# Low-rank weight products and the first rotations change engines in the opening stretch of a decoder kernel

## The reference, cut to what matters

```python
k = (c_kv @ Wk_up)...                      # and q = x @ Wq
q_rope, k_rope = _apply_rope(q_rope, ...), _apply_rope(k_rope, ...)
...
gate = einsum('btd,edf->ebtf', x, Wg)
gate = gate.at[:NL].add(einsum('btd,edr,erf->ebtf', x, Ga, Gb))   # up and out likewise, NL = 2, r = 64
```

## Time and profile before

| | before |
|---|---|
| median of 3 runs | 1698.6 us (1692.5 to 1699.74) |
| the profiled execution's own time | 1692.4 us |
| its span | 1690.6 us |
| PE busy | 1443.2 us, 85% |
| DVE busy | 1273.0 us, 75% |
| ACT busy | 903.6 us, 53% |
| POOL busy | 846.8 us, 50% |

### The profile page before, as it was taken

One profiled execution on the slowest core, in us unless ns is written; L12 is line 12 of the kernel. 1 busy time (PEld: TensorE's weight loads), 2 busy tenths in 40 slices (PEclk: granted clock), 3 DMA queues, 4 the chain that ended last, 5 costly groups with the idle time before them and its releaser, 6 DMA issues.

```text
span 1690.6 us, 26867 instructions
## 1 busy us (share of the span) xinstructions
PE 1443.2 (85%) x9924; PEld 869.5 (51%) x9924; DVE 1273.0 (75%) x2115; ACT 903.6 (53%) x1431; POOL 846.8 (50%) x724
## 2 busy tenths in 40 slices
...
GB/s 282 26 200 2 28 51 2 28 26 27 100 51 50 26 70 32 51 63 13 25 26 38 26 26 29 35 26 26 37 26 31 33 26 26 38 26 26 13 1 100
DMA packets 63105, 74.62 MB, mean 44 GB/s; under 512 B 6912, under 2 KB 40320, under 8 KB 61952
## 3 DMA queue, kind: packets, MB, share of 16 engines
...
## 4 chain that ended last, share of the span: by engine, by line
PE 60%; DVE 24%; issue 11%; ACT 3%; POOL 2%; DMA 1%; SPq 0%; DVEq 0%; POOLq 0%; ACTq 0%
PE banks L1103 48%; PE banks L870 6%; DVE nmf L1473 5%; DVE plo L1487 2%; PE banks L935 1%; DVE cat L1456 1%; PE banks L923 1%; DVE top L1599 1%; DVE wk L1595 1%; DVE att L1497 1%; DVE kcT L1463 1%; DMA w_fold<-w_top 1%; DVE attf L1606 1%; PE banks L1058 1%; DVE qcT L1483 1%
## 5 line engine op out<-in xcount | busy, mean ns | idle before, releaser
L1103 PE MATMUL banks<-xc,w 128*128 128x512 f16 x2688 | 591.2, 382 | 17.7 <-ACT banks L1144 15.0
L1103 PEld LDWEIGHTS banks<-xc,w 128*128 128x128 f16 x2688 | 264.2, 99 | 339.2 <-ACT banks L1144 20.2
L1103 PE MATMUL banks<-wd,mid 128*128 128x256 f16 x2688 | 298.1, 273 | 5.4 <-ACT banks L1144 3.1
L1103 PEld LDWEIGHTS banks<-wd,mid 128*128 128x128 f16 x2688 | 263.6, 98 | 40.9 <-ACT banks L1144 3.4
L847 POOL TENSOR_TENSOR mid<-m,mid 128x512 f16<-128x512 f32 x64 | 75.1, 1174 | 318.2 <-ACT mid L1144 318.2
L753 POOL TENSOR_TENSOR plo<-pf,phi 128x896 f16<-128x896 f32 x64 | 133.5, 2088 | 175.3 <-ACT phi L1144 175.2
L1144 ACT ACTIVATE banks<-banks 128x512 f32<-128x512 f32 x192 | 108.7, 579 | 193.0 <-PE banks L1103 193.0
L847 POOL TENSOR_TENSOR mid<-msum,mid 128x512 f16<-128x512 f32 x128 | 186.4, 1475 | 2.6 <-ACT mid L1144 2.6
L1421 DVE SCALAR_TENSOR_TENSOR w<-stage,w 128x512 f16<-128x512 f32 (+1 forms) x56 | 61.5, 1138 | 106.0 <-ACT w L1144 106.0
L1144 ACT ACTIVATE mid<-msum 128x512 f16<-128x512 f32 x128 | 81.2, 635 | 84.1 <-DVE msum L1780 28.1
L1473 DVE TENSOR_REDUCE nmf<-banks 128x1 f32<-128x512 f32 (+3 forms) x256 | 107.3, 480 | 14.9 <-PE banks L937 14.4
...
## 6 DMA issues: line engine op xcount, KB each, us to landing
...
```

The costliest lines, as they stand in the source:

```text
L1103: mm = nc.tensor.matmul(out, l(x, i), r(y, i), start=start and i == 0 and j == 0, stop=stop and i == k - 1 and j == 2, skip_group_check=True)
```

## The change

Six things change, all in the opening stretch.

1. The table in `kcT` is made in a small tile `own_small` of 4x16 and then spread to 4x8192 by one POOL copy.
2. A product leaves PSUM by ACT: `move_product` copies the four banks, scaled, into `product[n % 2]`, which lies in `pf` or in the new tile `low_high` (the old `phi` and `plo` in one). PE's next product waits for these copies (`lora_out`).
3. POOL adds a product to its weight with one instruction of 128x2048 (`lora_added` now counts 6, not 24). ACT's `move_product(n)` waits for the add of product n-2, and ACT's first batch waits for all six.
4. The eight rotations of the first batch are DVE's: `turn_row` has POOL's four instructions. Later batches keep POOL's.
5. The three tables of the opening stretch are written in another order.
6. The five later stores go in order 1 to 5, and each pair of factors shares a semaphore.

```diff
 A_START_PE = steps("""
-    xT.0 xT.1 xT.2 xT.3 turn.0 turn.1 row.0 c.0 row.1 fold.0 row.2 v.0 row.3 turn.2 fold.1 row.4 v.1 turn.3 fold.2 v.2
-    row.5 turn.4 fold.3 row.6 turn.5 fold.4 row.7 fold.5
+    xT.0 xT.1 xT.2 xT.3 turn.0 turn.1 row.0 c.0 fold.0 row.1 row.2 turn.2 v.0 row.3 fold.1 turn.3 row.4 v.1 fold.2 turn.4 row.5
+    v.2 row.6 fold.3 turn.5 row.7 fold.4 fold.5
 """)
 A_START_ACT = steps("""
-    fold.0 fold.1 row.0 c.0 row.1 rhi.0 row.2 rhi.1 row.3 v.0 fold.2 rhi.2 row.4 rhi.3 v.1 fold.3 v.2 row.5 rhi.4 fold.4
-    row.6 rhi.5 fold.5 row.7 rhi.6 rhi.7 v.3
+    half.0 half.1 row.0 c.0 row.1 rhi.0 fold.0 row.2 rhi.1 half.2 row.3 v.0 fold.1 rhi.2 row.4 half.3 rhi.3 v.1 fold.2 row.5 v.2
+    half.4 rhi.4 fold.3 row.6 half.5 rhi.5 row.7 rhi.6 fold.4 rhi.7 fold.5 v.3
 """)
 A_START_DVE = steps("""
-    half.0 half.1 c.0 rlo.0 rlo.1 fold.0 v.0 rlo.2 half.2 fold.1 v.1 rlo.3 half.3 fold.2 v.2 rlo.4 half.4 fold.3 rlo.5
-    half.5 fold.4 fold.5 cat0.0 cat0.1 cat0.2 cat0.3 cat0.4 rlo.6 cat0.5 rlo.7 cat0.6 cat0.7 maxn.0 maxn.1 maxn.2
-    maxn.3 v.3 mTn.0 maxn.4
+    half.0 half.1 rope.0 c.0 rope.1 rlo.0 half.2 v.0 rope.2 rlo.1 rope.3 rlo.2 half.3 v.1 rope.4 rlo.3 half.4
+    v.2 rope.5 rlo.4 rope.6 rlo.5 half.5 rope.7 cat0.0 rlo.6 cat0.1 cat0.2 cat0.3 rlo.7 cat0.4 cat0.5 cat0.6 cat0.7 maxn.0 maxn.1 maxn.2 maxn.3 v.3 mTn.0 maxn.4
 """)
...
         nm16 = sb(sa, "nm16", [P, TT, P], F16)
+        own_small = sb(sa, "own_small", [P, H], F16)
         qcT = sb(sa, "qcT", [P, H, S], F16)
...
         pf = sb(sa, "pf", [P, 2, TRI])
-        phi = sb(sa, "phi", [P, 2, TRI], F16)
-        plo = sb(sa, "plo", [P, 2, TRI], F16)
+        low_high = sb(sa, "low_high", [P, 4, TRI], F16)
+        phi, plo = low_high[:, 0:2], low_high[:, 2:4]
         osb = sb(sa, "osb", [P, 2, G, TT, 65])
...
         w_cat = vcat[:, :, :, :].rearrange("p h t n -> p (h t n)").bitcast(F32)[:, 0:2048].rearrange("p (t n) -> p t n", t=4)
+        product = [raw.rearrange("p a n -> p (a n)")[:, 0:2048].rearrange("p (t n) -> p t n", t=4) for raw in (pf[:, :, :], low_high[:, :, :].bitcast(F32))]
         w_raw = [w_cat, w_top[:, 0], w_top[:, 1], w_top[:, 2], x_res[:, :, :], att[:, :, :]]
...
         x2_kept = sem("x2_kept")
-        la_loaded = [sem(f"la{n}_loaded") for n in range(6)]
-        lb_loaded = [sem(f"lb{n}_loaded") for n in range(6)]
+        factors_loaded = [sem(f"factors{n}_loaded") for n in range(6)]
         wf_loaded = [sem(f"wf{n}_loaded") for n in range(6)]
...
         lora_mm = sem("lora_mm")
+        lora_out = sem("lora_out")
         lora_added = sem("lora_added")
...
             move_values(0, 1)
-            for n in (5, 4, 1, 2, 3):
+            for n in range(1, 6):
                 store_fold(n)
...
 
-            own_row = kcT[K3:K3 + G, :, :].rearrange("p (g j) n -> p g j n", j=G)
+            own_row = own_small[K3:K3 + G, :].rearrange("p (g j) -> p g j", j=G)
             pool.wait_ge(consts, 14)
-            pool.memset(kcT[K3:K3 + G, :, :], 0.0).then_inc(own_rows, 1)
+            pool.memset(own_small[K3:K3 + G, :], 0.0).then_inc(own_rows, 1)
             pool.wait_ge(own_rows, 1)
             pool.affine_select(out=own_row, in_=own_row, compare_op=ALU.not_equal, fill=SNM, base=0,
-                               pattern=[[0, H // G], [-1, G], [0, S]], channel_multiplier=1).then_inc(own_rows, 1)
-
+                               pattern=[[0, H // G], [-1, G]], channel_multiplier=1).then_inc(own_rows, 1)
             pool.wait_ge(own_rows, 2)
+            nc.gpsimd.tensor_copy(kcT[K3:K3 + G, :, :], own_small[K3:K3 + G, :].unsqueeze(2).to_broadcast([G, H, S])).then_inc(own_rows, 1)
+            pool.wait_ge(own_rows, 3)
+            for n in range(6):
+                pool.wait_ge(wf_loaded[n], 16)
+                pool.wait_ge(lora_out, 4 * (n + 1))
+                nc.gpsimd.tensor_tensor(w_raw[n], w_raw[n], product[n % 2], ALU.add).then_inc(lora_added, 1)
             pool.wait_ge(cossin_loaded, 16)
...
 
-            heads(next_part(A_POOL, A_NEXT), None, 0)
             with pool.Fori(0, B - 1) as b:
...
             def turn_factor(n):
-                pe.wait_ge(la_loaded[n], 16)
+                pe.wait_ge(factors_loaded[n], 32)
                 if n >= 2:
...
                     if n:
-                        pe.wait_ge(lora_added, 4 * (n - 1) + t + 1)
+                        pe.wait_ge(lora_out, 4 * (n - 1) + t + 1)
                     three(banks[:, t, :], lambda x, i: laT[:, n % 2, x, ts], lambda y, i: lb16[:, n % 2, y, :], 1, lora_mm)
...
             at = next_part(A_PE, A_NEXT).index(("cat0", 0))
-            pe.wait_ge(lora_added, 24)
+            pe.wait_ge(lora_out, 24)
             heads(next_part(A_PE, A_NEXT), None, 0, [], at)
...
             def factor_halves(n):
-                act.wait_ge(lb_loaded[n], 16)
+                act.wait_ge(factors_loaded[n], 32)
                 if n >= 2:
...
 
+            def move_product(n):
+                if n == 0:
+                    act.wait_ge(w_lo, 4)
+                elif n >= 2:
+                    act.wait_ge(lora_added, n - 1)
+                for t in range(4):
+                    act.wait_ge(lora_mm, 4 * n + t + 1)
+                    scaled(product[n % 2][:, t], banks[:, t, :], 1.0 / (SW * SW)).then_inc(lora_out, 1)
+
             for u in A_START_ACT:
                 if u[0] == "fold":
-                    if u[1] == 2:
-                        act.wait_ge(w_lo, 4)
+                    move_product(u[1])
+                elif u[0] == "half":
                     factor_halves(u[1])
...
                     heads([u], None, 0)
+            act.wait_ge(lora_added, 6)
             heads(own_part(A_ACT, ("res", "ln")), 0, 1)
...
 
-            def add_product(n):
-                dve.wait_ge(wf_loaded[n], 16)
-                for t in range(4):
-                    dve.wait_ge(lora_mm, 4 * n + t + 1)
-                    stt(out=w_raw[n][:, t], in0=banks[:, t, :], scalar=1.0 / (SW * SW), in1=w_raw[n][:, t],
-                        op0=ALU.mult, op1=ALU.add).then_inc(lora_added, 1)
+            def turn_row(i):
+
+                t = i // 2
+                if i == 0:
+                    dve.wait_ge(cossin_loaded, 16)
+                dve.wait_ge(a_drained["row"], a_upto(0, ("row", i)))
+                dve.wait_ge(roped, i * 4 + FREE)
+                pair = rows[:, i % 4, :, NOPE:HD].rearrange("p h (i two) -> p h i two", two=2)
+                for j, dst in ((0, turn_a), (1, turn_b)):
+                    cs = cossin[:, j, t].unsqueeze(1).to_broadcast([P, H, ROPE // 2, 2])
+                    tt_(dst[:, :, :, :], pair, cs, ALU.mult).then_inc(roped, 1)
+                dve.wait_ge(roped, i * 4 + (2 + FREE))
+                half = NOPE + ROPE // 2
+                tt_(rows[:, i % 4, :, NOPE:half], turn_a[:, :, :, 0], turn_a[:, :, :, 1], ALU.subtract).then_inc(roped, 1)
+                tt_(rows[:, i % 4, :, half:HD], turn_b[:, :, :, 1], turn_b[:, :, :, 0], ALU.add).then_inc(roped, 1)
 
             for u in A_START_DVE:
-                if u[0] == "half":
+                if u[0] == "rope":
+                    turn_row(u[1])
+                elif u[0] == "half":
                     factor_lows(u[1])
-                elif u[0] == "fold":
-                    add_product(u[1])
                 else:
```

More of the change, by code:

```diff
@@ L592, in _ @@
                 la, lb = (a[name][n // 3] for name in LORA[n % 3])
-                sp.dma_start(la_raw[:, n], la.rearrange("(t p) r -> p t r", p=P)).then_inc(la_loaded[n], 16)
-                sp.dma_start(lb_raw[:, n], lb).then_inc(lb_loaded[n], 16)
+                sp.dma_start(la_raw[:, n], la.rearrange("(t p) r -> p t r", p=P)).then_inc(factors_loaded[n], 16)
+                sp.dma_start(lb_raw[:, n], lb).then_inc(factors_loaded[n], 16)
                 if n % 2:
@@ L612, in store_fold @@
             def store_fold(n):
-                sp.wait_ge(lora_added, 4 * (n + 1))
+                sp.wait_ge(lora_added, n + 1)
                 sp.dma_start(w_fold[n // 3, n % 3].rearrange("(t p) n -> p t n", p=P), w_raw[n])\
@@ L948, in heads @@
                         if i == 0:
-                            pe.wait_ge(own_rows, 2)
+                            pe.wait_ge(own_rows, 3)
                         if i % G == 0:
```

## The result

| | before | changed |
|---|---|---|
| median, same session | 1699.17 us (4 runs, 1692.5 to 1702.38) | 1715.76 us (4 runs, 1709.07 to 1720.67) |
| ratio of the two, 95% interval | | 1.0102 [1.0066, 1.0138] |
| the profiled execution | 1692.4 us, span 1690.6 | 1709.07 us, span 1707.3 |
| `v.3` drained | 90.75 | 111.60 |

The change makes the kernel slower by 1.0%, 16.6 us between the medians. The forecast was 12.4 us and 1708.2; 1715.76 is near the upper end of its range, 1697 to 1717. A second session gave the same kernel a median of 1717.46, just over that end, and 1.0117 [1.0092, 1.0143] of its own before.

A forecast was written before the change was run, and what follows sets the result against it. The prediction took the end of `v.3`, with five stores behind it in SyncE's queue, as the bound. Its terms, -5.6 -1.3 +14.7 +3.6 +1.0, gave +12.4 us on 1695.8: 1708.2 us, range 1697 to 1717.

The forecast's parts named there:

- term 1: Opening table: POOL's copy ends before DVE's `wq` starts, so `wq` ends at 18.5 instead of 24.15: -5.6 us.
- term 2: DVE's own work in the opening: 24 adds go (14.73 us), eight rotations come (13.4 us): -1.3 us.
- term 3: SBUF path shared by POOL and DVE: POOL's additions stop DVE's two-input operations, 18.0 us for 3.3 before: +14.7 us.
- term 4: DVE's idle time from `wq` to the last `cat0` copy: 17.1 us for 13.5 before: +3.6 us.
- term 5: TensorE's clock in the heads' maxima, a ring of PE and DVE: two early rounds also at 1.2 GHz: +1.0 us.
- What bounds it: Opening stretch: five stores stand behind `v.3` in SyncE's queue, so the time moves by as much as `v.3`'s end.
- slow copy: Rival on the opening table: POOL's copy takes 16.4 us, `wq` ends at 26.8, time 1716.5 us; chance 0.06.
- The base: Time the forecast change was added to: 1695.8 us, the mean of two pairs of executions of the kernel before.
- the stalls fall off the path in part: Rival: stalls at `half.2` and `rope.2` (6.2 us) are absorbed; sum +6.2, 1702 us, no telling change; chance 0.22.
- hold nothing: Rival: POOL's additions hold nothing that DVE needs, so no stalls; 1692 us, no change; chance 0.05.
- Faster: Rival: DVE's waits swallow all its stalls in the opening; -10.2 us, 1685.6 us; chance 0.07.
- The clock, inside the forecast: Rival: PE's clock falls in its 5.9 us gap before `row.6`, costing 1.3 to 2.5 us more; no chance given.

The follow-up runs named there:

- e9: The changed kernel with its five later stores issued ahead of SyncE's wait for `v.3`: 1699.33 us, 1.0005 of the kernel before.
- e2: The kernel before with its five later stores issued ahead of SyncE's wait for `v.3`: 1686.76 us, 0.9924 of the kernel before.
- e1: The kernel before with only the table's change (small tile, one spreading POOL copy): 1692.02 us, 0.9957 of the kernel before.
- e4: The changed kernel with each POOL addition split into four pieces of 128x512: 1711.82 us, 1.0079 of the kernel before.
- e6: The kernel before with the table's change and the first batch's rotations on DVE, additions still on DVE: 1704.22 us, 1.0037 of the kernel before.
- e7: The changed kernel with the rotations back on POOL, between its additions: 1712.94 us, 1.0103 of the kernel before.
- e3: The changed kernel with POOL's six additions replaced by memsets about as long, which only write SBUF: 1695.38 us, 0.9991 of the kernel before.
- e10: The changed kernel with 56 extra matmuls in three of PE's gaps, none ahead of `cat0.3`: 1700.99 us, 1.0029 of the kernel before.
- e5: The changed kernel with 74 extra matmuls in four of PE's gaps, results thrown away: 1708.08 us, 1.0051 of the kernel before.
- e11: The kernel before with the table's change, stores ahead of `v.3` and 36 extra matmuls in PE's gaps: 1668.47 us, 0.9834 of the kernel before.

## Why the prediction was right, and where it was off

| from | forecast | measured, profiled execution |
|---|---|---|
| term 1, table | -5.6 | -5.7 |
| term 2, DVE's own work | -1.3 | -1.9 |
| term 3, stalls | +14.7 | +10.5 |
| term 4, DVE's idle time | +3.6 | +16.5 |
| term 5, clock in the ring | +1.0 | +1.4 |
| end of `v.3` | +12.4 | +20.8 |

- **What bounds it** held for the change, though not only through the queue. `v.3` came 20.85 us later and DVE went on 20.83 later. The stores behind `v.3` are worth some 14 us of DVE's wait in either kernel (18.5 for 4.3 behind `v.3`, e9), but with them out of the way a later `v.3` still cost its time (e9 over e2: 12.6 us for 14.6), since the lists of DVE and PE have it ahead of the first batch. "The time moves by as much as `v.3`" holds within the scatter behind it for the changed kernel, 16.6 and 20.2 us in two sessions for 20.85 and 21.2, and for e1, e4, e6 and e7. It does not for e3 (-3.4 for +3.2), e10 (+3.8 for +16.7) and e5 (+9.3 for +20.8), and why is open.
- **Term 1** held in the changed kernel and alone (e1). The slow copy, 16.4 us, is out with 7.01.
- **Term 2**, here what is left of DVE's busy time when term 3 is taken off: a rotation is 0.55, 0.55, 0.36 and 0.35, overlapping, close to the estimate.
- **Term 3** was right in its mechanism (e3) and too high for this execution. In the groups of the stretch the eight `turn_a` have a mean of 1498 ns for 550, `cat` 1026 for 690, `kcT` 1252 for 673: 7.6, 2.7 and 3.5, together 13.8 against 18.0, less the 3.3 of before. The missing stall is that of `rlo.3`. It ran from 50.95 to 51.63, and addition 2, forecast at 51.0, came at 53.81, since `fold.2` was slow. In its place the first operation of `half.4` lost 0.9, and `rlo.6` lost 2.7 for 3.9. With the clock held, addition 2 comes at 51.14 and the stall is there. The additions took 4.50 to 4.59 where I had taken 4.4; the row of another shape with 9% for fp32 was a little low. The Trainium skill's 4497 ns for 2048 fp32 columns (GPSIMD Engine Reference, "Elementwise — side-by-side cycle accounting") was the closer figure, and the trace agrees with it; by it the sum of the prediction, by its own estimate, would have been 0.5 us more.
- **Term 4 is the step that failed.** "17.1" was 29.9. The forecast's wait for `half.2` (2.6) was met at 2.60; not forecast was the 5.62 ahead of `half.4`, the wait for `rope.6` was 7.15 for 4.5, and those in the `cat0` steps 9.1 for 4.7. In each of the three PE is at a product of 5.30 us. The prediction had named the gap and the price, "may cost 1.3 to 2.5 more", for one gap, and left it outside the sum. There were four gaps of 3.4 to 4.8 us, three of them right behind a stall, and three products of 2.76 took 2.54 more each, with shorter groups beside them. e5 and e10 show that this is the cause up to `cat0.0`: with the clock held it comes at 76.97, for 82.93 without, and `rlo.6` within 0.8 us of its place in the forecast. e10's DVE had 20.9 us of idle time, 3.8 over the forecast, 2.9 of it in the copies behind `cat0.0`, at the low clock. In the end of `v.3` e10 won back 4.2 of the 8.4 us that the forecast missed; most of the other half lies behind `cat0.0`, where no run held the clock.
- **Term 5** had the right rows and was 0.4 low: all three rounds between the four maxima took 3.45, the first maximum came 2.60 behind the last `cat0` copy's start for 1.88, and the 0.4 taken off for overlap wasn't there.
- **The base**: the mean of the four executions, 1695.8, was 3.4 under the median that the session gave, 1699.17. Both errors have one sign; together they are the 7.6 us between 1708.2 and 1715.76. That this lies inside the range is in part luck: `v.3` was 8.4 us past its forecast, and the first session gave 4.2 of them back in the scatter behind it. The second session's 1717.46 is half a microsecond outside.
- **The rivals**: that the stalls fall off the path in part, or hold nothing, is refuted by e3, which takes out only the reading and gets 17.6 us back. (Its "3.7 before today's `v.3`" can't be had from the terms, which give 12.4 - 18.0 = -5.6.) "Faster" is out. The clock, inside the forecast, was the one that came.

The parts of the change, by experiments, in the end of `v.3`: the table -5.6 (e1), all else without the additions' reading +8.9 (e3 less e1), the reading +17.6 (changed less e3): 20.9. By the other way, the rotations' move +11.9 (e6 less e1), and moving the products by ACT and adding them on POOL another +14.6. These are differences of single profiled executions, each with what its clock did: the +8.9 and the +11.9 both include a stretch at a lower clock (0.86 and 0.80 for e1's 0.97). What stays open is what makes the stretch behind `v.3` scatter by 11 us between two executions of one kernel, and why the extra matmuls of e5, e10 and e11 gain more in the medians than in the stretch where they stand.
